# Graph attention on one core: when ScalarE widens the one-hots, in which order it takes the exponentials, and what the scan waits for

## What is computed

```python
Qh, Kh, Vh = (x @ Wq + bq), (x @ Wk + bk), (x @ Wv + bv)      # (N, 8, 32)
s = einsum('nhc,nhc->nh', Qh, Kh) / sqrt(32)
src, dst = src + loops, dst + loops                            # each node also has an edge to itself
alpha = leaky_relu(s[src] + s[dst], 0.2)
m = segment_max(alpha, dst)
e = exp(alpha - m[dst])
a = e / segment_sum(e, dst)[dst]
attn = segment_sum(Vh[src] * a, dst)                           # (N, 256)
h = x + attn @ Wo + bo                                         # then batch norm
```

## Time and profile before

| | us |
|---|---|
| median of 3 runs | 4592.16 |
| the profiled execution's own time | 4596.53 |
| its span, first to last instruction | 4594.5 |
| attention stage within the span | 588 to 1809 |
| mean granted PE clock over the span | 0.891 |

### The profile page before, as it was taken

The page is one execution under the profiler, slowest core; times in us unless marked ns, Lnnn a source line. Parts: engine busy times, 40 slices in busy tenths (PEclk is TensorE's granted clock), DMA queues, the critical chain, the costliest instruction groups (busy, mean ns, idle before and its releaser), DMA issues. The chain is left out here.

```text
span 4594.5 us, 70306 instructions
## 1 busy us (share of the span) xinstructions
PE 3626.4 (79%) x16651; PEld 2353.7 (51%) x16652; DVE 2077.2 (45%) x7633; ACT 1232.0 (27%) x2424; POOL 2630.5 (57%) x2830
## 2 busy tenths in 40 slices
PE   3877746666666667975999998788888888588998
PEld 1223335555555555864777776343343343367776
DVE  6976657777777775354222221222222222333332
ACT  3973322222222222254333333000000000122222
POOL 4001166666666663023666664777777777477775
PEclk9999967777777777975999999899999999799999
DMA  4431133333333331046888876777777777666675
GB/s 150 168 139 51 49 98 103 103 106 104 103 103 103 106 104 50 0 116 188 239 244 245 248 234 184 217 225 230 226 226 230 226 226 229 176 203 205 201 211 167
DMA packets 352403, 750.64 MB, mean 163 GB/s; under 512 B 82289, under 2 KB 161183, under 8 KB 348872
## 3 DMA queue, kind: packets, MB, share of 16 engines
q0 software_dynamic: 208336, 538.34, 41.3%
q10 hardware_dynamic: 72332, 112.04, 7.7%
q1 hardware_dynamic: 71529, 98.27, 6.5%
HBM read 654.57 MB, written 93.84 MB: 163 GB/s over the span
## 5 line engine op out<-in xcount | busy, mean ns | idle before, releaser
L1695 POOL DMA_INDIRECT l_gathered<-table,record x850 | 818.7, 963 | 399.5 <-issue 277.3
L780 POOL DMA_INDIRECT a_gathered<-table,record x850 | 812.3, 956 | 386.5 <-issue 263.9
L2055 POOL DMA_INDIRECT l_gathered<-table,record x850 | 814.4, 958 | 302.0 <-issue 296.2
L2149 PE MATMUL bank<-l_gathered,l_onehot 128*125 128x512 f32 x1700 | 811.2, 628 | 161.7 <-DMA l_gathered<-table,record 161.4
L2149 PEld LDWEIGHTS bank<-l_gathered,l_onehot 128*125 128x125 f32 x1700 | 325.2, 197 | 620.9 <-issue 357.4
L1110 PE MATMUL bank<-a_gathered,a_onehot 128*125 128x264 f32 x1700 | 517.9, 458 | 111.1 <-DVE a_gathered L908 111.1
L1825 ACT ACTIVATE l_part<-l_packed 128x1000 fp32r<-128x1000 bf16 (+1 forms) x300 | 314.2, 1072 | 530.1 <-PE bank L1906 427.6
L1110 PEld LDWEIGHTS bank<-a_gathered,a_onehot 128*125 128x125 f32 x1700 | 357.2, 221 | 193.1 <-DVE a_gathered L908 67.1
L1925 PE MATMUL bank<-l_gathered,l_onehot 128*125 128x256 f32 (+1 forms) x1275 | 329.3, 415 | 86.0 <-DMA l_gathered<-table,record 86.0
L2088 DVE SCALAR_TENSOR_TENSOR l_z<-l_own,one_eps,bank 125x512 f32<-125x512 f32 x50 | 37.3, 747 | 707.3 <-PE bank L2156 707.3
L1906 PE MATMUL bank<-rows_first,l_part 125*125 125x512 f32 x1250 | 307.5, 405 | 28.6 <-ACT l_part L1825 28.6
(11 more groups left out here) (265 smaller groups left out, 5042.4 us busy)
## 6 DMA issues: line engine op xcount, KB each, us to landing
l_packed<-adjacency ACTq DMA_DIRECT2D x200, 250.0 KB, 4.9
adjacency<-d_stage SPq DMA_DIRECT2D x25, 1562.5 KB
l_packed<-adjacency ACTq DMA_DIRECT2D x100, 281.2 KB, 5.8
l_gathered<-table,record POOLq DMA_INDIRECT x1700, 3.7
a_gathered<-table,record POOLq DMA_INDIRECT x850
table<-rows_first POOLq DMA_DIRECT2D x50, 250.0 KB, 3.3
table<-l_work ACTq DMA_DIRECT2D x50, 250.0 KB
l_own<-table SPq DMA_DIRECT2D x50, 250.0 KB
```

The costliest lines, as they stand in the source:

```text
L780: pool.indirect_dma_start(out=gathered0[s][:, j * TW:(j + 1) * TW], out_offset=None, in_=table0, in_offset=bass.IndirectOffsetOnAxis(ap=re ...
L1695: pool.indirect_dma_start(out=gathered[g][:, j, :], out_offset=None, in_=table, in_offset=bass.IndirectOffsetOnAxis(ap=record[k.t][:, j, 0 ...
L2055: pool.indirect_dma_start(out=gathered[s][:, j * w:(j + 1) * w], out_offset=None, in_=table, in_offset=bass.IndirectOffsetOnAxis(ap=record ...
L2149: last = pe.matmul(sum_ps[s][0:NB, 0:w], onehot[s][:, j, :], rows[:, j, :], start=False, stop=(j == T - 1), skip_group_check=True)
```

## The change

DVE's first wait in `scores_of` becomes a wait for a new semaphore `reset_ready`, which ACT's reset copy (L1025) raises. ACT's `widen` leaves the end of the previous block's round and goes into the block's own round, behind `self_exp` and ahead of `begin_block`. In `weights` the exponentials into PSUM come first, then those into the gathered rows with a new semaphore `sums_weighed`, then run_m. PE's `sums` of quarter 0 waits for `sums_weighed` as well.

```diff
@@ scores_of (DVE)
-                    dve.wait_ge(prepared[s], r)
+                    dve.wait_ge(reset_ready[s], r)
                     dve.wait_ge(rows_gathered[s], r * GATHERED)
@@ prepare_reset (ACT)
-                    act.activation(reset[s][:, :, 1:T], rec[:, 1:T, 2].unsqueeze(1).broadcast_to([P, HEADS, T - 1]), ACT.Copy)
+                    act.activation(reset[s][:, :, 1:T], rec[:, 1:T, 2].unsqueeze(1).broadcast_to([P, HEADS, T - 1]),
+                                   ACT.Copy).then_inc(reset_ready[s], 1)
@@ weights (ACT)
-                    act.activation(run_m[s][:, :], node_m[s][:, :], ACT.Copy)
-                    act.activation(rows[:, :, D:TW], alpha2[s][:, :, :], ACT.Exp)
                     act.activation(node_ps[s][:, FACTOR:FACTOR + T * HEADS].rearrange("p (j h) -> p j h", h=HEADS), alpha2[s][:, :, :],
                                    ACT.Exp).then_inc(weights_ready[s], 1)
+                    act.activation(rows[:, :, D:TW], alpha2[s][:, :, :], ACT.Exp).then_inc(sums_weighed[s], 1)
+                    act.activation(run_m[s][:, :], node_m[s][:, :], ACT.Copy)
@@ first_round (ACT)
                     if before is not None:
                         self_exp(*before)
+                    widen(s)
                     begin_block(s, i)
@@
                     if before is not None:
                         copy_attended(*before)
-                    if after is not None:
-                        widen(after[0])
@@ ahead of over_blocks (ACT)
                 prepare_reset(0)
                 prepare(0)
-                widen(0)
@@ sums (PE)
                     if q == 0:
                         pe.wait_ge(onehot_wide[s], r)
+                        pe.wait_ge(sums_weighed[s], r)
                         pe.wait_ge(block_done[s], i + 1)
```

More of the change, by code:

```diff
@@ L667, in build @@
                                                                       pair("weights_ready"))
-            weighted, block_begun = pair("weighted"), pair("block_begun")
+            weighted, block_begun, reset_ready, sums_weighed = (pair("weighted"), pair("block_begun"), pair("reset_ready"),
+                                                               pair("sums_weighed"))
             self_loaded, self_shifted, self_weight = pair("self_loaded"), pair("self_shifted"), pair("self_weight")
```

## The result

The changed kernel takes 4557.89 us (median of 4 runs, 4552.48 to 4565.14) against 4592.32 us before: a ratio of 0.9922, 95% interval 0.9908 to 0.9937. It is faster, by 34 us where I forecast 55; the time lies within my range. The runs of the changed kernel differ by up to 13 us; those of the kernel before differed by 0.8 us here. The page of the changed kernel begins with

The account below looks back on a forecast made before the run. A circular chain of waits through the attention blocks, 23.89 us each, was taken to bound the kernel. 0.97 + 0.32 = 1.29 us over 49 distances gave 63 us, less 8 for the clock: -55 us, 4537 us, range 4508 to 4572.

Parts of the forecast that it names:

- my own sum: Attention blocks: 0.97 us from the widening plus 0.32 us from the exponentials, 1.29 us a block, 63 us over 49 distances.
- or if L919 still waits: Sign that the prediction is wrong: DVE's L919 keeps its 1.64 us wait for ACT instead of a few tenths.
- What bounds the kernel: Attention loop: one circular chain of waits sets 23.89 us a block; time moves by 49 times what it loses.
- Scan behind the reset alone: DVE's L847 no longer waits for the turned one-hots: worth nothing alone, bounds 0 and 0.67 us.
- Exponentials first: ACT's exponentials into PSUM start where L1050 did, so DVE's weighing L908 starts sooner: -0.32 us a block.
- Widening behind the own weight: ACT reaches the own weight's exponential at T+7.3, L919 starts near T+7.6, L854 at T+10.46: -0.97 us a block.
- The clock, -63 to -55 us: PE's low-clock stretch stops recurring in step with the attention blocks: a loss of 8 us over the stage.
- Rival 1: The rise of PE's clock holds the block distance and takes back half to all the gain: 4560 to 4592 us, chance 0.17.
- Rival 2: PE idles less, so quarter 0 runs at the high clock in half the blocks: 82 us, 4510 us, chance 0.15.
- Rival 3: PE's low clock covers projection and quarter 1 too: +1.5 us a block, 73 us slower, 4665 us, chance 0.03.
- Rival 4: Another wait than ACT's, such as the gathered rows, holds L919 or L854: nothing changes, 4592 us, chance 0.03.
- POOL: Next resource: 17 gathers, 21.3 us a block; its wait for PE shrinks from 2.62 to about 1.3 us, rows still covered.

Follow-up runs that it names:

- the first experiment: The kernel before with only the exponentials reordered, plus PE's wait for sums_weighed: 4578.13 us (7 runs), ratio 0.9965.
- the filled kernel: The changed kernel with matmuls of zeros in PE's two idle stretches of each block: 4472.25 us, ratio 0.9735.

## Why the prediction was right, and where it was not

The direction and the range held. The working held less well than the total says, and in part it was luck: with the widening at its measured 0.20 us my own sum is 0.52 x 49 = 25 us, less 8 for the clock, which gives about 4575 us, just outside my range. What brought it inside is 0.09 us a block behind L855, which no step of mine has, and the clock, which I had as a loss. By my own signs the widening's step failed ("or if L919 still waits").

- **What bounds the kernel**: right. The circle of waits and the 49 distances carry the result: from the first to the last instruction of the weighings are 1168.9 us before and 1134.1 us after (623.9 to 1758.0 us), 34.8 us less in the profiled executions.
- **Scan behind the reset alone, worth 0**: right, shown by undoing it (0.9918 against 0.9922).
- **Exponentials first, -0.32 us**: the size is right, 0.66 to 0.35 us of waiting. That it is paid in full is not: alone it gave between nothing and 21 us, by the execution, 14.6 by the median.
- **Widening behind the own weight, -0.97 us**: here the prediction failed. The step says "ACT now reaches the own weight's exponential behind L1061, at T+7.3". It came at T+8.85, and L855 gained 0.2 us, not 0.97. In the kernel before the widening was more than 1.97 us of work in the way: it was the cover under which ACT got through its loads of first_edge, its test and its branch. There L1057 starts as the widening ends, with no gap:

```profile
1228.93 1.97 ACT L1042 ACTIVATE a_onehot<-a_onehot_bf 128x2125 f32<-128x2125 bf16 x1
1230.80 0.20 ACT L1057 ACTIVATE a_selfw<-a_selfw 125x8 f32<-125x8 f32 x1
```

  I had asked what the moved work would be late for, and not what it had been hiding. The kernel without that control work has the step as I wrote it, L920 at T+7.66 and PE's L1132 ahead of L855 at T+10.54, and its time, 69 us below before, is near my sum of 63 us; as its clock moves too, the two agree in part by chance. The Trainium skill ("Perfetto Trace Analysis", Per-instruction lifecycle, DVE / Act Engine Instruction) draws the sequencer as ready for its next instruction once one is pushed to the queue behind it; with that picture control work is free under a long instruction and bare behind a short one, and the traces here agree: no gap ahead of L1057 behind 1.97 us of widening, 1.38 us ahead of L1059 behind the copy. A sign was in the trace of before: in blocks of one set DVE itself idled between its last weighing and L914 with no releaser, which I passed over. That this is DVE's own loads is not tested.

```profile
1227.88 0.17 DVE L914 TENSOR_TENSOR a_selfw<-self_alpha,a_node_m 125x8 f32<-125x8 f32 x1 [1.29 <-issue]
```

- **The clock, -63 to -55 us**: the 8 us were a guess, and the mechanism is larger than it. The waits alone gave 0.6 us in a block whose clock rises about where it did before (23.86 to 23.25 us: 0.20 up to L855, 0.41 from there on). In the repeating four the mean distance fell by 0.86 us; the other 0.26 us stand in the blocks with an early rise. Over all 49 distances it fell by 34.8 / 49 = 0.71 us, since the blocks of 24.5 us near the start took part of it back. So, as an estimate from these rows, the clock added about 5 us on the way to 34 us where I had it take 8.
- **Rival 1, the clock takes the gain back**: wrong for the whole change, right for its parts. The constant 23.89 us were indeed not the chain's own length alone: 0.78 us more waiting per block left it as it was. With 0.3 us less, in the profiled execution of the first experiment, the single distances changed and their mean did not: the rise moved behind the projection and into quarter 1, as this rival has it, but in one block of three. The Trainium skill ("TensorE: Matmul & The Clock Gate", Part 1: The HAM clock gate) says that PE's activity is what releases the clock. The rises here agree as far as they all come within or behind the sums of quarter 0; but with eight copies these sums start at T+1.27 as before, and the rise comes at T+4.3 instead of T+6.7, so the start of the sums alone does not fix it. What decides between a swallowed and a paid 0.3 us is not settled.
- **Rival 2, the clock gives more**: right in kind; the filled kernel shows its full size, 86 us below the changed one.
- **Rival 3, slower**: not for the change. Its mechanism, the projection and quarter 1 at the low clock, is there in single blocks: in the block of 24.34 us above the projection takes 2.07 us instead of 1.16 and quarter 1 2.70 us instead of 1.95, and it is 1.5 to 1.7 us longer than its neighbours (22.69 and 22.84 us). I had put 0.9 and 1.93 us on the two; in full the second would need a rise behind all of quarter 1.
- **Rival 4, another wait holds L919**: no. The gathered rows held L848 for 17.1 us in 22 blocks, and L920 waited for ACT behind it each time.
- **POOL**: the arrival of the rows was right, 1233.88 - 1231.05 = 2.83 us from the start of the last gather to the copy. Its wait for PE fell from 2.7 to 2.2 us a block, not to 1.3, since the block is longer than forecast; without ACT's control work it is 1.4 us. Its floor of 21.3 us is where the filled kernel stands.

## What to carry to other kernels

Before moving a long instruction off a path, look at what the engine's sequencer does behind it: here the loads of loop bounds, the test and the branch cost nothing under 1.97 us of widening and 1.4 to 1.6 us behind a copy of 0.38 us, nearly all of it the loads. Hoisting the loads ahead of a wait that is long anyway brought about 30 us more (ratio 0.9853 against 0.9922). In a loop whose distances are constant to a few hundredths while PE's clock falls and rises at one place in each, a small saving or cost on the path may not show at all, so a null result there does not mean that the edit was off the path: look at the single distances and at the clock, not only at the time. Keeping PE busy through its idle stretches was worth more (86 us) than the whole change.

## What the runs showed of the hardware that was not expected

- Eight extra copies on ACT, 0.78 us on the path of each of 49 blocks, some 38 us in all, left the time as it was (ratio 1.0003, 0.9993 to 1.0012), while the mean granted clock rose from 0.89 to 0.91.
- One kernel has executions 25 us apart (4571.73 to 4597.27 us) on one chip; the kernel before stays within 9 us on that chip.
- Two loads of first_edge and the work around them hold ACT for 1.4 to 1.6 us; with the loads moved away, 0 to 0.3 us are left.
- Matmuls of zeros in PE's idle stretches kept the granted clock at 1.00 over 950 us, where it was 0.82 without them.
- One chip ran the kernel before in 6009 us instead of 4592 us, with its engines standing still up to 29 us at a time.
